# Keys in token order, one value load a batch, and mask rows in two parts: a two-layer decoder on one core

## The reference, cut to what matters

```python
xk = jnp.einsum('bsh,oh->bso', x, wk)
xk = xk.reshape(bsz, N_HEADS, seqlen, HEAD_DIM)
scores = jnp.einsum('bhid,bhjd->bhij', xq, xk) * SCALE
out = jnp.einsum('bhij,bhjd->bhid', jax.nn.softmax(scores, axis=-1), xv)
```

## Time and profile before

| | us |
|---|---|
| median of 3 runs | 285.77 |
| lowest and highest of the 3 | 284.87, 710.45 |
| the profiled execution | 287.07 |
| its span | 285.3 |
| PE busy in the span | 232.6 (82%) |
| DVE busy | 200.9 (70%) |
| ACT busy | 153.7 (54%) |

### The profile page before, as it was taken

How to read it: one execution, slowest core, us unless ns; L and a number is a source line. 1 busy time by engine, 2 the same in 40 slices (tenths; PEclk the granted TensorE clock), 3 DMA queues, 4 the chain that set the end, 5 groups by cost and what they waited for, 6 DMA issues and landing times.

```text
span 285.3 us, 6881 instructions
## 1 busy us (share of the span) xinstructions
PE 232.6 (82%) x2662; PEld 186.8 (65%) x2662; DVE 200.9 (70%) x535; ACT 153.7 (54%) x288; POOL 61.2 (21%) x108
## 2 busy tenths in 40 slices
PE   1869889989899999997994979979998887765442
PEld 1737767879698896986873847757765755453221
DVE  2695996479855989756443547567777878778896
ACT  4983765385737866463544125645643266551372
POOL 4698000000003001030212031443520101011133
PEclk9959999999999999999998689999999999987555
DMA  6265496147763471044979917920040000000002
GB/s 190 105 147 186 100 241 254 62 105 165 208 186 104 102 167 76 3 124 92 247 194 155 231 28 153 187 68 2 15 107 0 3 3 0 2 0 0 0 10 64
DMA packets 28495, 29.15 MB, mean 102 GB/s; under 512 B 19248, under 2 KB 24496, under 8 KB 27184
## 3 DMA queue, kind: packets, MB, share of 16 engines
q1 hardware_dynamic: 28464, 28.72, 39.6%
HBM read 18.49 MB, written 6.03 MB: 86 GB/s over the span
## 4 chain that ended last, share of the span: by engine, by line
PE 47%; DVE 25%; DMA 8%; ACT 6%; issue 6%; SPq 6%; POOL 1%; POOLq 0%; DVEq 0%
DVE arena L1305 7%; DMA k_piece<-VN 4%; PE PS L665 4%; SPq L390 4%; ACT arena L1056 3%; PE PS L799 3%; PE PS L589 3%; PE PS L692 3%; PE PS L782 2%; PE PS L633 2%; DMA arena<-q_piece 2%; PE PS L779 2%; PE PS L780 2%; PE PS L610 2%; DVE arena L1480 2%
## 5 line engine op out<-in xcount | busy, mean ns | idle before, releaser
L1305 DVE TENSOR_TENSOR arena<-PS,arena 64x512 f16<-64x512 f32 x64 | 44.1, 690 | 9.8 <-ACT arena L1056 8.5
L1056 ACT ACTIVATE arena<-PS 64x512 f16<-64x512 f32 x64 | 37.8, 591 | 11.7 <-PE PS L620 10.6
L494 POOL TENSOR_SCALAR shift<-mv 128x3 f32<-128x3 f32 (+2 forms) x12 | 2.9, 241 | 161.4 <-DVE mv L1357 161.4
L1145 ACT ACTIVATE PT<-PS 128x512 f32<-128x512 f32 x32 | 19.0, 594 | 19.9 <-PE PS L783 19.5
L1442 DVE TENSOR_REDUCE rowmax<-PS 128x4 f32<-128x512 f32 x32 | 21.7, 682 | 10.8 <-PE PS L783 10.7
L618 PE MATMUL PS<-xh,w0l 128*128 128x256 f32 x64 | 20.8, 324 | 7.8 <-DVE w0l L1296 5.7
L665 PE MATMUL PS<-V,PT 128*64 128x68 f32 x512 | 22.7, 232 | 3.0 <-issue 1.8
L1310 DVE TENSOR_REDUCE rowmax<-PS 128x4 f32<-128x512 f32 x32 | 21.7, 683 | 2.9 <-PE PS L634 2.5
L1069 ACT ACTIVATE PT<-PS 128x512 f32<-128x512 f32 x32 | 19.0, 595 | 8.7 <-PE PS L649 7.6
L647 PE MATMUL PS<-arena 128*128 128x128 f16 x128 | 23.3, 221 | 0.1
L649 PE MATMUL PS<-MR,En 128*128 128x128 f16 x128 | 23.1, 219 | 0.0
(11 more groups left out here) (229 smaller groups left out, 631.7 us busy)
## 6 DMA issues: line engine op xcount, KB each, us to landing
arena<-later SPq DMA_DIRECT2D x4, 1152.0 KB, 10.7
arena<-arena SPq DMA_DIRECT2D x8, 512.0 KB, 5.4
v_piece<-VN SPq DMA_DIRECT2D x8, 512.0 KB, 3.0
V<-v_piece SPq DMA_DIRECT2D x64, 64.0 KB, 2.5
V<-later SPq DMA_DIRECT2D x2, 768.0 KB, 10.9
arena<-k_piece SPq DMA_DIRECT2D x4, 192.0 KB, 4.8
arena<-q_piece SPq DMA_DIRECT2D x4, 192.0 KB, 6.0
q_piece<-VN SPq DMA_DIRECT2D x6, 96.0 KB, 5.7
```

Of the source, the lines that this page charges most:

```text
L1056: m = fn(dst[:, a], src[a * 64:(a + 1) * 64], ACT.Copy)
L1305: m = tt(lower[:, a], src[a * 64:(a + 1) * 64], upper[:, a], ALU.subtract)
```

## The change

1. `by_column` gets a flag for keys: their columns stand as (t, a, g). In the writes of L1056 and L1305 for i = 0 to 3, consecutive tokens are then 16 fp16 (32 bytes) apart. Queries stay as they are.
2. With row j of a head on partition j, a batch's values come back by one load of 512 KB, so 2 loads a pair instead of 16.
3. The mask rows are loaded in parts, as the batches under them leave: group 0's first half (three loads) ahead of pair 3's value stores, once 20 score groups have left, its second half after pair 3's value loads and 24 groups; group 1's halves after 28 and 32; group 2's in two parts as well. `stack_in` counts 10, 10 and 7 transfers.

```diff
-        def by_column(buf, i):
+        def by_column(buf, i, keys=False):
 
-            v = buf.rearrange("p (n a g t) -> p a g n t", a=2, g=G, t=8)
+            order = "n t a g" if keys else "n a g t"
+            v = buf.rearrange(f"p ({order}) -> p a g n t", a=2, g=G, t=8)
             return v[:, :, 2 * (i % 4):2 * (i % 4) + 2, :, :]
...
-            return s(f"v_load{p % 2}{q // 4}"), 128 * (p // 2 + 1)
+            return s(f"v_load{p % 2}{q // 4}"), 16 * (p // 2 + 1)
...
+            def mask_rows(h, keys, queries):
+
+                for i, x, cols in ((0, Kst[h], keys), (1, Qst[h], queries)):
+                    for a, z in cols:
+                        sp.dma_start(x[EDGE:P].rearrange("p n t -> p (n t)")[:, a:z], later[i, :, a:z])\
+                            .then_inc(s(f"stack_in{h}"), 16)
+
+            def mask_half(h, at):
+
+                o = 2048 * at
+                mask_rows(h, ((o, o + 2048),) + (((4096, 6144),) if at == 0 else ()),
+                          ((2048, 4096),) if at == 0 else ((0, 2048), (4096, 6144)))
...
+                if p == 3:
+                    sp.wait_ge(s("sk_done"), NQ - 12)
+                    mask_half(0, 0)
...
                     if p >= 2:
                         sp.wait_ge(s("pv_done"), QP * (p - 1))
-                    for t in range(8):
-                        sp.dma_start(V[t::8, b, h * H:(h + 1) * H, 0:DH0],
-                                     v_piece[2 * p + h].rearrange("n (t c) d -> t c n d", t=8)[t])\
-                            .then_inc(s(f"v_load{b}{h}"), 16)
-            for h in MIDS:
-                cols = slice(B0[h] * P, (B0[h] + N[h]) * P)
-                sp.wait_ge(*((s("sk_done"), 24), (s("sk_done"), NQ), (s("pv_done"), NQ))[h])
-                for i, x in enumerate((Kst[h], Qst[h])):
-                    sp.dma_start(x[EDGE:P].rearrange("p n t -> p (n t)"), later[i, :, 0:H * N[h] * P])\
-                        .then_inc(s(f"stack_in{h}"), 16)
...
+                    sp.dma_start(V[:, b, h * H:(h + 1) * H, 0:DH0], v_piece[2 * p + h].rearrange("n j d -> j n d"))\
+                        .then_inc(s(f"v_load{b}{h}"), 16)
+            sp.wait_ge(s("sk_done"), NQ - 8)
+            mask_half(0, 1)
+            pieces(0)
+            sp.wait_ge(s("sk_done"), NQ - 4)
+            mask_half(1, 0)
+            sp.wait_ge(s("pv_done"), 24)
+            mask_rows(2, ((0, 4096),), ((0, 2048),))
+            sp.wait_ge(s("sk_done"), NQ)
+            mask_half(1, 1)
+            pieces(1)
+            sp.wait_ge(s("pv_done"), NQ)
+            mask_rows(2, (), ((2048, 4096),))
+            pieces(2)
...
-                pe.wait_ge(s(f"stack_in{g}"), 96)
+                pe.wait_ge(s(f"stack_in{g}"), (160, 160, 112)[g])
...
-                    dst = by_column((KA, QS)[i // 4][p % 2][0:64, :], i)
+                    dst = by_column((KA, QS)[i // 4][p % 2][0:64, :], i, i < 4)
...
-                upper, lower = (by_column((KA, QS)[i // 4][p % 2][x, :], i) for x in (slice(0, 64), slice(64, P)))
+                upper, lower = (by_column((KA, QS)[i // 4][p % 2][x, :], i, i < 4) for x in (slice(0, 64), slice(64, P)))
```

More of the change, by code:

```diff
@@ L346, in _, with pieces @@
                     sp.dma_start(w0[:, i, cols], w[:, cols]).then_inc(s(name + str(j)), 16)
+            def mask_rows(h, keys, queries):
[7 more added lines that the diff above has]
+                          ((2048, 4096),) if at == 0 else ((0, 2048), (4096, 6144)))
+            def pieces(h):
+                cols = slice(B0[h] * P, (B0[h] + N[h]) * P)
+                for hi_or_lo, slot, src in (("kp_hi", 0, kph), ("kp_lo", 1, kpl)):
+                    sp.wait_ge(s(hi_or_lo), h + 1)
+                    sp.dma_start(k_piece[h][slot], src[:, cols]).then_inc(s("k_out"), 16)
+                for hi_or_lo, slot, src in (("qp_hi", 0, qph), ("qp_hi", 2, qph), ("qp_lo", 1, qpl)):
+                    sp.wait_ge(s(hi_or_lo), h + 1)
+                    sp.dma_start(q_piece[h][slot], src[:, cols]).then_inc(s("q_out"), 16)
+                sp.wait_ge(s("k_out"), 32 * (h + 1))
+                for r in range(2):
+                    sp.dma_start(rows(Kst[h], r), k_piece[h].rearrange("i (d n) t -> (i d) (n t)", d=DH1))\
+                        .then_inc(s(f"stack_in{h}"), 16)
+                sp.wait_ge(s("q_out"), 48 * (h + 1))
+                for r in range(2):
+                    sp.dma_start(rows(Qst[h], r), q_piece[h][r:r + 2].rearrange("i (d n) t -> (i d) (n t)", d=DH1))\
+                        .then_inc(s(f"stack_in{h}"), 16)
             def load_first():
@@ L351, in load_first, with load_late @@
                 sp.dma_start(xt[:], x_tok).then_inc(s("ld_wo"), 16)
+            def load_late():
                 sp.dma_start(wgu_s[:], wgu).then_inc(s("ld_late"), 16)
@@ L378, in _ @@
                     load_first()
+                    load_late()
                 if p == 2:
                     load_rest()
+                if p == 3:
+                    sp.wait_ge(s("sk_done"), NQ - 12)
+                    mask_half(0, 0)
                 for h in range(2):
```

## The result

| | before | after |
|---|---|---|
| median | 285.32 us | 352.75 us (350.62 to 353.46, 4 runs) |
| ratio, with its 95% interval | | 1.2376 [1.2287, 1.2465] |
| profiled execution, its span | 287.07, 285.3 | 350.62, 348.8 |

One of the four runs of the kernel before took 710.45 us, and the ratio goes by the means of the others. The changed kernel is 24% slower. I had forecast 280.8 us with 278.8 to 297.0 as the range, so the sign, the size and the range were wrong. The new file's lines are shifted: L1056 is now L1082, L1305 is L1331, the value loads are L427, `weigh` is L691, the expert product L775, the first product of a keys' or queries' projection L644, that of a values' projection L636.

A forecast was written before the change was run, and what follows sets the result against it. PE was taken to set most of the pace and DVE part, the change aiming at the rest. From 287.07 us, -1.8 - 2.3 - 0.9 + 0 = -5.0 gave 282.1, or 280.8 us on the median's scale; range 278.8 to 297.0.

The forecast's parts named there:

- The layout of the keys: Key writes of ACT's L1056 and DVE's L1305, now lone fp16 32 bytes apart: taken to cost zero.
- The upper bound: Key writes at twice the price per element: 532 ns an instruction on DVE, at most 17 us, some 15.5 after gaps.
- ACT's share lies beside DVE's: Key writes in the projections: ACT's extra time runs alongside DVE's, so only DVE's was priced.
- The value loads: PE's wait before L665 near 130 us, from pair 3's sixteen loads, goes with two: -1.8 us.
- Rival 3: Waits only change names: the 512 KB load takes as long as eight, clock falls: -2.3, 283.5 us; 0.10 with rival 4.
- The stack: PE's 3.42 us wait for the second attention's query rows goes, but group 1's layer norm is late next: -2.3 us.
- some 2: The new gap on PE, in us, waiting for group 1's layer norm rows before transposes L709.
- the later stacks are worth nothing: Masks of groups 1 and 2 move earlier, but PE never waited for those stacks: no gain.
- The clock: Group 1's product L749 runs at full clock, 0.86 us against 1.73, after a shorter PE gap: -0.9 us.
- The sum without the layout: Whole kernel with the key layout at zero: -5.0 us, giving 280.8 us on the median's scale.
- Rival 1: Scattered key writes at L1305 and L1056 cost full price: +15.5 against -5.0, 296.3 us; chance 0.31.
- Rivals 2 and 4: 2: scattered writes at half rival 1's price, +7.8, 288.6 us, 0.12. 4: masks still ahead of pieces, 0.10 with rival 3.

The follow-up runs named there:

- the keys in pairs: The changed kernel with ACT's and DVE's key writes walked column block innermost, so that two adjacent fp16 are written right after each other: 280.36 us, ratio 0.9807.
- the first experiment: The changed kernel with keys written in their old order, all else of the change kept (wrong rows mixed): 279.2 us, ratio 0.9819.
- two others: Old keys, masks in parts, 16 value loads a pair: 281.23 us; the same with the first batch's loads ahead of the second's store from pair 1: 279.42 us.

## Why the prediction was wrong

**The layout of the keys** is the step that failed: "I take zero, since DVE's own rows are nearer than POOL's, and keep both ends." Two faults are in it.

The rows taken as nearest had no lone elements of two bytes. L1430's runs of 8 floats are 32 bytes at a time, where nothing is to be seen, and the reciprocal had four elements. I noted both and still gave them the weight. The rule of the Trainium skill ("Advanced Engine Details and Errata", section "Memory Cachelines": 16-byte lines, at least two hits on each, else a penalty) was the better guide. The fp32 rows agree with it: lone fp32 16 bytes apart take 1.06 us against 0.69, and 8 bytes apart 0.69. The fp16 rows don't bear it out in full: lone fp16 8 bytes apart hit each line twice and still take 1.29, and there the measurement decides.

The upper bound was no bound. "Twice the price per element" came from POOL's fills of fp32, and gave 532 ns an instruction. Measured are 2.31 - 0.69 = 1.62 us on DVE and 2.31 - 0.59 = 1.72 on ACT. A doubling in fp32 on another engine says nothing on two-byte writes. With no row of the operation, its end had to lie much farther out.

**"ACT's share lies beside DVE's"** failed as well. It held for the old durations only, where ACT had slack. With 2.3 us each, either engine alone costs 53.4 us, and ACT adds 19 us to DVE's. With the true price of one instruction, the prediction's own sum (32 of DVE, the rest beside) would have given 280.8 + 52 = 333 us, so this step was worth 19 of the 72 us missed.

**What held.** To leave out small shifts at the start of a run, I compare from the end of group 0's expert product (start + length) to that of group 1's: before 161.62 - 118.07 = 43.55 us. After that, in the kernel with the layout undone, product 0 starts at 115.97 and product 1 ends at 155.51: 155.51 - 116.83 = 38.68, which is -4.9, against the forecast -5.0; that these agree so well is in part luck, since the clock gave less than I had. With masks only it starts at 116.27 and the second ends at 158.23: 158.23 - 117.13 = 41.10, or -2.45, against the -2.3 of the stack alone (-3.2 with the clock). By terms:

- The value loads, -1.8: right. The two kernels just compared differ by 41.10 - 38.68 = 2.42 us, of which 1.72 - 1.08 = 0.64 is the clock. The new load lands in 4.9 us (forecast 4.5), and the wait was still gone. Rival 3's 4.9 is the same number by luck, since 10.7 x 512 / 1152 is 4.8. SP's two issues took 3.47 us where I had about 1, and that wasn't waited for either. The page of the kernel after:

```profile
V<-v_piece SPq DMA_DIRECT2D x8, 512.0 KB, 4.9
```

- The stack, -2.3 of 3.4: right, and the layer norm is late next. The waits before L735 and L775 are 1.07 and 0.30 us where I had "some 2". That the later stacks are worth nothing held with the layout undone, but not with the keys in pairs (1.12 us).
- The clock, -0.9: partly. The product takes 1.08 us in the first experiment, 1.32 with the keys in pairs, and 1.72 in two others, never 0.86. The clock still falls to 0.50, the 1.2 GHz level, at about that place: a stretch of the kernel with the layout undone shows it, in the columns used above.

```profile
156.00:158.00 2.00, 1.85 (x11) 1.52 (x10) 1.90 (x8) 0.81 (x2) 0.00 (x0) 0.50 0.00 0
```

  The fall only comes later or earlier against the product. I had reasoned from one gap of 2 us at a time, but here three short ones (0.62, 1.07, 0.30 us) come within 4 us before it; that they bring the fall wasn't tested. So the term is 0 to -0.65.
- The sum without the layout, 280.8: measured 279.2 and, with the keys in pairs, 280.36.
- Rival 1 had the right mechanism and place, at a fifth of the true cost: +15.5 instead of +72 us. Rivals 2 and 4 fall. Rival 3 falls as a whole, since the wait for V was gone, but its half on the clock came about in the two kernels with 1.72 us.

## What to carry to other kernels

Before a change of layout, ask in which order in time the elements of one instruction fall into each 16 bytes: keep neighbours in memory neighbours in the innermost loop, and write fp16 at least two neighbours at a time. Where the trace has no row for an access pattern, rows of another width or engine don't bound it; measure it alone first. If an instruction that empties PSUM becomes longer, price every engine in its ring (ACT, then DVE, then PE), since slack in a ring covers only what fits in it.

## What the runs showed of the hardware

- A 64 x 512 write of lone fp16, 16 or more bytes apart, takes 2.29 to 2.43 us on DVE and on ACT, against 0.69 and 0.60 adjacent. For fp32 it is 1.01 to 1.09.
- Two fp16 adjacent in memory but written two elements apart in time cost as much as lone ones (2.50 us, against 0.69 when written right after each other).
- Reads cost less: lone fp16, 32 bytes apart, take 0.62 against 0.43 us on DVE, 1.13 against 0.64 on ACT.
- SP needs 3.5 us to issue pair 3's values as two loads of 512 KB, and 11.2 us as sixteen of 64 KB; the bytes and the 256-byte pieces are the same.
